# The seven loads of a weight table's deep levels issued ahead of the thirty-one of its upper levels

## What is computed

```python
h = tok_ref(x, ...)                       # pooled attention over 4x4 patches: 32 x 256 tokens of 64
h = h + attn_ref(layernorm(h), ...)       # gated linear scan over the 256 tokens of each image
h = h + ffn_ref(layernorm(h), ...)        # a binary tree of 255 nodes, depth 8

# ffn_ref, for each token:
current = 0
for i in range(8):                        # root to leaf
    score = x . w1s[current] + b1s[current]
    path_weight = gelu(|score|)
    out += (x @ w2s[current] + b2s[current]) * path_weight     # a 64 x 64 matrix of that node
    current = 2 * current + 1 + (score > 0)
```

## Time and profile before

| | |
|---|---|
| runs | 620.93 us median of 3 (620.38 to 623.08) |
| profiled execution, span from the first to the last instruction | 621.0 us |
| PE, DVE, ACT, POOL busy | 93%, 84%, 72%, 72% of the span |
| granted clock of TensorE, mean over the span | 0.981 |
| HBM | 50.19 MB read, 10.28 MB written |
| SP's queue of DMAs (q1) | 44120 packets, 49.23 MB |
| POOL's queue of DMAs (q0) | 5120 packets, 6.99 MB |

### The profile page before, as it was taken

How to read it: one execution, slowest core, us unless ns; L and a number is a source line. 1 busy time by engine, 2 the same in 40 slices (tenths; PEclk the granted TensorE clock), 3 DMA queues, 4 the chain that set the end, 5 groups by cost and what they waited for, 6 DMA issues and landing times. The chain is left out here.

```text
span 621.0 us, 15981 instructions
## 1 busy us (share of the span) xinstructions
PE 579.8 (93%) x5276; PEld 306.2 (49%) x5276; DVE 524.2 (84%) x1029; ACT 448.5 (72%) x936; POOL 447.6 (72%) x458
## 2 busy tenths in 40 slices
PE   7999999999999999999768997999868999999995
PEld 4223333333333333333235664666536888888884
DVE  3599999999999999999765885989988888888883
ACT  4887778777877777786247986888856777777772
POOL 5957988899889889955765153566677767667676
PEclk9999999999999999999889998999998999999999
DMA  7432333332223333000008498111114333322200
GB/s 275 158 141 115 136 137 137 137 122 73 95 121 137 136 137 136 20 1 12 4 0 217 97 166 142 53 36 39 35 53 115 80 86 84 81 71 69 73 21 1
DMA packets 49602, 58.19 MB, mean 94 GB/s; under 512 B 31932, under 2 KB 44836, under 8 KB 47544
## 3 DMA queue, kind: packets, MB, share of 16 engines
q1 hardware_dynamic: 44120, 49.23, 26.3%
q0 software_dynamic: 5120, 6.99, 3.6%
q10 hardware_dynamic: 288, 1.05, 0.4%
HBM read 50.19 MB, written 10.28 MB: 97 GB/s over the span
## 5 line engine op out<-in xcount | busy, mean ns | idle before, releaser
L831 PE MATMUL s_proj<-x_px,w_kv 64*64 64x512 f32 x256 | 130.5, 602 | 0.9 <-DVE qk L607 0.9
L837 PE MATMUL s_proj<-x_px,w_kv 64*64 64x512 f32 x256 | 130.6, 602 | 0.0
L2164 POOL DMA_INDIRECT out<-orow,m_rows x96 | 94.5, 984 | 40.5 <-issue 34.4
L1264 POOL DMA_INDIRECT rows_by_group<-r_pay,r_slot_i x64 | 65.7, 1026 | 47.7 <-ACT r_pay L1406 9.1
L501 POOL TENSOR_TENSOR half_px<-x_px 128x1024 f32<-128x1024 f32 x30 | 71.3, 2377 | 29.8 <-DMA x_px<-in_x 29.8
L522 POOL TENSOR_TENSOR pre<-va 128x1024 f32<-128x1024 f32 x32 | 76.2, 2382 | 21.8 <-DVE va L623 20.0
L607 DVE TENSOR_TENSOR qk<-s_proj,q 128x512 f32<-128x512 f32 x128 | 85.4, 678 | 5.0 <-PE s_proj L837 2.8
L623 DVE TENSOR_TENSOR va<-b_a,v_sb 128x1024 f32<-128x1024 f32 x62 | 75.6, 1219 | 7.5 <-PE b_a L875 7.5
L317 ACT ACTIVATE x_sq<-x_px 128x1024 f32<-128x1024 f32 x64 | 67.2, 1050 | 18.6 <-PE b_x L912 18.6
L2133 PE MATMUL s_delta<-m_xsT,m_w_cur 128*64 128x128 f32 x1152 | 71.1, 273 | 0.0
L831 PEld LDWEIGHTS s_proj<-x_px,w_kv 64*64 64x64 f32 x256 | 31.5, 134 | 74.0 <-issue 52.3
(11 more groups left out here) (318 smaller groups left out, 1746.8 us busy)
## 6 DMA issues: line engine op xcount, KB each, us to landing
x_px<-in_x SPq DMA_DIRECT2D x15, 2048.0 KB, 7.6
m_rows<-rows_by_group SPq DMA_DIRECT2D x96, 72.0 KB
wt<-in_w2T SPq DMA_DIRECT2D x8, 512.0 KB
rows_by_group<-rows_by_group SPq DMA_DIRECT2D x1, 2286.0 KB, 9.6
out<-orow,m_rows POOLq DMA_INDIRECT x96, 2.3
x_px<-in_x ACTq DMA_DIRECT2D x2, 512.0 KB, 5.9
x_px<-in_x SPq DMA_DIRECT2D x2, 512.0 KB, 7.1
rows_by_group<-r_pay,r_slot_i POOLq DMA_INDIRECT x64
```

The lines of the kernel that those rows point to most:

```text
L831: mm(b_k[i][LO, :], w_kv[LO, 0, :], px(t, j, LO), start=True, stop=True)
L837: mm(b_k[i][HI, :], w_kv[HI, 0, :], px(t, j, HI), start=True, stop=True).then_inc(done["kv_product"], 1)
L1264: g.indirect_dma_start(rows_d, bass.IndirectOffsetOnAxis(ap=slot_i[:, c % 2, k:k + 1], axis=0), pay[:, c % 2, k, :], None).then_inc(scatte ...
L2164: nc.gpsimd.indirect_dma_start(out_d, bass.IndirectOffsetOnAxis(ap=rows[:, i, ID0:ID0 + 1].bitcast(I32), axis=0), orow[:, i, :], None, bou ...
```

## The change

In SP's block the load of level 5 and the six loads of levels 6 and 7 move ahead of the loop over levels 0 to 4. The loop loses its case for level 5. The same 62 loads are issued on the same queue and semaphore, and the biases stay last.

```diff
         w2 = A["w2T"]
-        for l in range(6):
-            k, side = l // 2, l % 2
-            n0, cn = 2 ** l - 1, 2 ** l
-            if l == 5:
-                ld(wt[half(side), :, k + 1, :], w2[:, n0:n0 + cn, :])
-                continue
-            r = GRP // cn
-            for v in range(cn):
-                ld(wt[half(side), v * r:(v + 1) * r, k + 1, :], w2[:, n0 + v:n0 + v + 1, :].broadcast_to([C, r, C]))
+        ld(wt[half(1), :, 3, :], w2[:, 31:63, :])
         for side in range(2):
             ld(wt[half(side), :, 4, :], w2[:, 63:127, :].rearrange("d (g u) o -> d g u o", u=2)[:, :, side, :])
             for m in range(2):
                 ld(wt[half(side), :, 5 + m, :], w2[:, 127:255, :].rearrange("d (g u) o -> d g u o", u=4)[:, :, 2 * m + side, :])
+        for l in range(5):
+            k, side = l // 2, l % 2
+            n0, cn = 2 ** l - 1, 2 ** l
+            r = GRP // cn
+            for v in range(cn):
+                ld(wt[half(side), v * r:(v + 1) * r, k + 1, :], w2[:, n0 + v:n0 + v + 1, :].broadcast_to([C, r, C]))
```

## The result

The changed kernel takes 617.28 us (median of 7 runs, 616.45 to 619.47) against 623.08 us (median of 7, 620.38 to 625.03) for the kernel before in the same comparison. The ratio is 0.9932, with a 95% interval of 0.9906 to 0.9958: faster, by 0.7%, or 4.2 us of 621, with 2.6 to 5.8 us inside the interval. The two medians lie 5.8 us apart, at the upper end of it. Forecast were 615.3 us and a gain of 5.65 us. The direction and the mechanism held, and the time came out 2.0 us higher.

The account below looks back on a forecast made before the run. PE, busy 93% of the span, was taken to stand still once through ACT's wait for a scatter delayed by large loads. Median 620.93 less 5.65, other terms 0, gave 615.3 us; 8 in 10 range 614.0 to 618.4.

Parts of the forecast that it names:

- What bounds the kernel, and what goes: ACT L1397 (`keep_h`, chunk 2) waits 4.2 us for chunk 0's eighth scatter, late beside large loads; the wait goes.
- The large loads first cost nothing: Seven large loads at the head of SP's loads, heavy part ending between 362 and 370: cost 0.
- either rate assumed: DMA rates for the heavy part: 178 GB/s (337 to 346) and 209 GB/s (361.6 to 382), giving 25 to 29 us.
- The upper levels beside the scatter: Small loads of levels 3 and 4 meet the eighth scatter at 374.52 instead of the large ones: no wait.
- The bound of 3.26 us: Chunk 1's eighth scatter, issued at 396.72, landed within this, against 3.36 us available from 374.52 to 377.88.
- The rule that the prediction set against the change: Skill's advice to coalesce transfers under 64 KB; read strictly, 32 KB loads hold the engines as long: no gain or worse.
- Rivals B and C: B: queue still full at 374.52, 621 us, chance 0.10. C: small loads delay two scatters, 626.6 us, chance 0.07.
- What the event costs in all: One scan chunk step of 22.19 us against a mean of 16.54: 5.65 us lost, by ACT's wait and a restart.
- the second part (1.56 us): Restart after PE stood still 3.92 us: granted clock 0.61 between 382 and 386, costing at most 1.56 us.
- A: The forecast case: one chunk step of 16.5 where 22.19 stood, gain 4.2 to 5.8 us, chance 0.78.
- The base: Profiled span of 621.0 us taken as 0.1 over the median of 620.93, from which the gain was subtracted.
- That it arrives whole: After the scan nothing is tied to a fixed time, so all 5.65 us reach the end.

Follow-up runs that it names:

- the third buffer: Kernel before with its load order kept, but `pay` given three buffers instead of two, against the kernel before: ratio 0.9940 (0.9916 to 0.9964).
- the second trace: The changed kernel, unchanged, traced a second time: 617.40 us, span 615.7.
- four loads first: Four of the large loads ahead of the upper levels, three behind them, against the kernel before: ratio 0.9981 (0.9950 to 1.0012).
- two more loads: Order of before with two more never-read 512 KB loads behind the seven, against the kernel before: ratio 1.0025 (1.0002 to 1.0047).
- third trace of before: The kernel before, unchanged, traced a third time: 621.58 us, span 619.8.
- first trace: The kernel before as profiled for the prediction, span 621.0 us, median 620.93 us.

## Why the prediction was right, and where it was wrong

*What bounds the kernel, and what goes.* Right. The one wait of ACT was the whole event: the third buffer removes it with the loads untouched and gives a time that the intervals do not tell from the changed kernel's, and moving the loads moves it.

*The large loads first cost nothing.* Right. The step beside them, from 355.58 to 372.07, is 16.49 us, and the third buffer's steps are 16.48 to 16.51 at a share of 1.33. The heavy part was for a stretch slower than either rate assumed, 158 GB/s between 347 and 361.4, and ended just past the range, at about 371 instead of 362 to 370. One reading on the way was wrong, with no weight in the sum: the 17.15 us from 361.01 to 378.16 belong to six large loads and not to seven, 2.86 us each; the first of the seven went out at 360.37, in 0.61 us.

*The upper levels beside the scatter.* Right, but with next to no room. The bound of 3.26 us is when ACT was ready in a quiet chunk, not when the scatter landed, so it could not show room against 3.36. In the two traces of the changed kernel ACT stood 0.15 and 0.31 us ahead of L1395; in the quiet chunk, and with the third buffer, the line starts 0.1 us before the one ahead of it ends. Those tenths may be what is left of the wait; the profile names no releaser for them. The rule that the prediction set against the change is answered by the same rows: beside small loads the scatter took at most 3.50 us at share 0.32, and at most 3.66 in the second trace, beside a full queue of 512 KB loads 5.14 to 7.56. Rivals B and C, and with them a strict reading of that rule, did not come about.

*What the event costs in all.* This step failed in its size: the term of 5.65 us was read from one execution and stood for all. Three traces have 5.68, 4.50 and 1.85, mean 4.0; the one at hand was the largest. The third buffer, which takes away the same wait, gains 3.7 us, and its interval of 2.2 to 5.2 leaves 5.65 out. The changed kernel's own ratio, 4.2 us with 2.6 to 5.8, agrees with the mean but does not leave 5.65 out. Two things differ from execution to execution: the time a scatter takes beside large loads, and whether the clock falls while PE stands still, which the sum counted as part of the price. The sum noticed the second part (1.56 us) and had it in hand. The wait alone, 4.20 us, stood in it as the lower end of the range for A; as a value it would have been near, but by luck, since the three waits are 4.20, 3.34 and 2.02.

*The base.* This term failed too. The text set the span of 621.0 beside the median of 620.93 and took the two for one quantity. They are not: 1.7 to 1.9 us lie outside the span in every run that has both on record (617.48 against 615.7 in the changed kernel's trace). So the traced execution of before took about 622.8 us, an estimate, and was slower than two of the three runs shown. With four more runs the median of before rose to 623.08; in the comparisons that came later it was 622.14 (35 runs), 622.60 (11) and 620.90 (13). From 622.8 the sum would have given 622.8 - 5.65 = 617.2, where 617.28 was measured. The size alone nearly closes the 2.0 us as well: 620.93 less the mean loss of 4.0 is 616.9. Both mended together give 618.8, too much, so that 617.2 comes so near is in part luck. Which of the two weighs more in this comparison stays open: its medians, 5.8 us apart, speak for the base, its ratio for the size.

*That it arrives whole.* Right within the trace: from the pair at 355.13 to the end there were 265.9 us, now 260.1 from the pair at 355.58, 5.8 less, which is the lost 5.68 of that trace.

## What to carry to other kernels

When a wait for a DMA is on the path, ask what else fills the DMA engines at that moment: moving bulk loads to where nobody waits for a DMA takes the wait away without taking any work away, and one more buffer does the same. A stall that depends on two streams meeting differs from execution to execution, so its size wants several traces. That an engine started without idle time only bounds what it might have waited for; it does not show how much room is left. Check first how the traced execution's time stands to the median, with what lies outside the span added.

## What the runs showed of the hardware

A 72 KB scatter took at most 3.3 to 3.7 us from its start beside small loads; it took 3.96 us beside a single 512 KB load and 5.1 to 7.6 us beside a full queue of them. Two more loads behind it changed nothing (6.32 us). A 512 KB load issued alone, after the one before had landed, went out every 4.95 us and took SP 0.60 us to issue; in a full queue six of them took SP 2.86 us each (361.01 to 378.16 in the earlier trace rows).

The granted clock did not follow the length of PE's standing still alone: after 3.92 and 3.05 us it was 0.61 and 0.69 on average over the next 4 us (a mix of 1.2 and 2.4 GHz), after 3.43 us (four loads first), 2.68 us (two more loads) and 1.74 us (third trace of before) it stayed at 1.00. At the start of the scan 1.96 us of standing still were followed by 0.57 between 334 and 338 (third trace of before), and 1.56 us by 1.00 (first trace). What decides stays open.
